# First layer of a four-layer block: two 32-token blocks swapped in every second tile, and a block-wise triangular solve in three stages over four diagonal array tiles

## What is computed

```python
q = silu(x @ Wq.T); k = silu(x @ Wk.T); v = x @ Wv.T        # 16 heads of 32
beta = 2.0 * sigmoid(x @ Wbeta.T)
k = k * rsqrt(sum(k * k) + EPS)
def step(S, inp):                                            # one token after the other
    qt, kt, vt, bt = inp
    pred = einsum('bhk,bhkv->bhv', kt, S)
    delta = bt[..., None] * (vt - pred)
    S = S + einsum('bhk,bhv->bhkv', kt, delta)
    o = einsum('bhk,bhkv->bhv', qt, S)
    return (S, o)
gate = sigmoid(x @ Wg1.T @ Wg2.T); og = o * gate
og = og * rsqrt(mean(og * og) + EPS) * g_norm;  return og @ Wo.T
```

## Time and profile before

| | us |
|---|---|
| median of three runs | 4828.01 (4825.08 to 4836.86) |
| the profiled execution, its own time | 4826.68 |
| its span in the profile | 4824.6 |
| first layer, start of the span to about | 1860 |
| mean granted clock of TensorE | 0.978 of full speed |

### The profile page before, as it was taken

How to read it: one execution, slowest core, us unless ns; L and a number is a source line. 1 busy time by engine, 2 the same in 40 slices (tenths; PEclk the granted TensorE clock), 3 DMA queues, 4 the chain that set the end, 5 groups by cost and what they waited for, 6 DMA issues and landing times.

```text
span 4824.6 us, 144788 instructions
## 1 busy us (share of the span) xinstructions
PE 4466.7 (93%) x63104; PEld 3089.8 (64%) x63104; DVE 3603.4 (75%) x7890; ACT 2416.7 (50%) x4592; POOL 707.2 (15%) x909
## 2 busy tenths in 40 slices
PE   7999999999999985999999999999999999999998
PEld 6777777777887764565565565565565565565564
DVE  5777767777777773877877877877877877877876
ACT  3344444434444332646646646646646646645645
POOL 0000000000000001122122122122122122122121
PEclk8999999999999997999999999999999999999999
DMA  2223222222322222000000000000000000000000
GB/s 88 56 74 75 73 69 65 65 69 74 78 69 65 65 65 80 1 18 1 19 18 2 19 19 2 19 19 2 19 18 2 19 18 2 19 18 2 19 10 10
DMA packets 352135, 171.76 MB, mean 36 GB/s; under 512 B 300017, under 2 KB 300785, under 8 KB 350737
## 3 DMA queue, kind: packets, MB, share of 16 engines
q1 hardware_dynamic: 342528, 145.20, 11.3%
q10 hardware_dynamic: 8976, 17.30, 1.3%
HBM read 93.74 MB, written 67.63 MB: 33 GB/s over the span
## 4 chain that ended last, share of the span: by engine, by line
PE 45%; DVE 11%; ACT 2%; issue 1%; POOL 1%; DMA 1%; SPq 0%; DVEq 0%; ACTq 0%; POOLq 0%
PE row_psum L1720 10%; PE row_psum L1745 10%; PE row_psum L40 5%; PE row_psum L42 5%; PE row_psum L41 5%; DVE smax L2007 5%; PE row_psum L1733 4%; PE row_psum L1793 1%; DVE xr_lo L1868 1%; PE row_psum L1773 1%; DVE probs L1987 1%; PE row_psum L1507 1%; DVE stats L1834 1%; POOL rstd L1304 1%; PE row_psum L1692 1%
## 5 line engine op out<-in xcount | busy, mean ns | idle before, releaser
L2007 DVE TENSOR_REDUCE smax<-row_psum 128x1 f32<-128x512 f32 x2048 | 1270.5, 681 | 94.8 <-PE row_psum L1720 93.7
L1441 ACT ACTIVATE probs<-row_psum 128x512 f32<-128x512 f32 x2048 | 1090.7, 602 | 350.0 <-PE row_psum L1733 330.5
L1720 PE MATMUL row_psum<-k_stack,q_stack 64*128 64x512 f32 (+1 forms) x2048 | 740.5, 440 | 50.6 <-DVE smax L2007 24.4
L1733 PE MATMUL row_psum<-q_stack,k_stack 64*128 64x512 f32 (+1 forms) x2048 | 733.5, 458 | 20.3 <-ACT probs L1441 8.1
L1720 PEld LDWEIGHTS row_psum<-k_stack,q_stack 64*128 64x128 f32 (+1 forms) x2048 | 354.3, 188 | 499.3 <-DVE smax L2007 367.9
L1745 PE MATMUL row_psum<-probs,v_aug 128*32 128x512 f32 x4096 | 538.9, 603 | 1.7 <-ACT av_sb L1457 0.4
L1733 PEld LDWEIGHTS row_psum<-q_stack,k_stack 64*128 64x128 f32 (+1 forms) x2048 | 319.2, 184 | 223.3 <-ACT probs L1441 155.7
L894 DVE TENSOR_TENSOR lane_t<-lane_t,lane_p 128x30 f32<-128x30 f32 (+14 forms) x960 | 318.3, 332 | 33.0
L40 PE MATMUL row_psum<-wf_hi,xr_hi 128*128 128x320 f32 (+1 forms) x1024 | 332.0, 324 | 5.3 <-DVE xr_lo L1868 3.2
L891 DVE TENSOR_TENSOR lane_p<-lane_t 128x30 f32<-128x30 f32 (+14 forms) x960 | 316.0, 329 | 25.5
L42 PE MATMUL row_psum<-wf_hi,xr_lo 128*128 128x320 f32 (+1 forms) x1024 | 319.0, 312 | 0.0
(11 more groups left out here) (215 smaller groups left out, 9854.2 us busy)
## 6 DMA issues: line engine op xcount, KB each, us to landing
x_sp<-in_x ACTq DMA_DIRECT2D x33, 512.0 KB, 4.3
tri_dram<-tri SPq DMA_DIRECT2D x256, 64.0 KB, 3.2
lane_t<-tri_dram SPq DMA_DIRECT2D x32, 512.0 KB, 3.8
inv_dram<-lane_t SPq DMA_DIRECT2D x32, 512.0 KB, 2.7
inv_b<-inv_dram SPq DMA_DIRECT2D x256, 64.0 KB, 2.3
x_res<-in_x SPq DMA_DIRECT2D x32, 512.0 KB, 3.9
x<-x_res SPq DMA_DIRECT2D x32, 512.0 KB, 3.2
xs<-x SPq DMA_DIRECT2D x16, 1024.0 KB, 5.5
```

The costliest lines, as they stand in the source:

```text
L1441: act.activation(probs[:, h % PROBS, tt, :], ps[:, m % STACK_BANKS, :], ACT.Exp, scale=float(DH) ** -0.5).then_inc(exp_ready, 1)
L1720: pe.matmul(ps[:, bank, :], q_stack[rows, qt, P * st:P * st + P], k_stack[rows, kv, :], start=True, stop=True).then_inc(max_mm, 1)
L1733: pe.matmul(ps[:, m % STACK_BANKS, :], k_stack[rows, kv, P * tt:P * tt + P], q_stack[rows, qt, :], start=True, stop=True).then_inc(score_m ...
L2007: dve.tensor_reduce(smax[:, g, st:st + 1], ps[:, bank_of("max", NT * g + st), :], AX.X, ALU.max).then_inc(max_ready, 1)
```

## The change

Tile 1 of every span gets its two 32-token blocks swapped in each chunk: its early block now lies on partitions 32 to 63 and 96 to 127. `upper` of tile 1 then uses array tiles (1,1) and (3,3), `product` (1,0) and (3,2), `under` (0,0) and (2,2). The four solve stages become three, `solve_upper`, `solve_product` and `solve_under`, each with all four quarters (128 records), in which tile 0's and tile 1's matmuls alternate: four array tiles with no row and no column in common.

- `turned` does tile 1's four blocks as fp32 matmuls with a swapped identity where it had transposes.
- The queries and the gate go back to token order when ScalarE reads them: `take_q` and `take_gate` become three activations for each one (256, 128 and 128 elements a partition).
- Tile 1's triangles use a swapped mask. The swapped identity and mask are loaded by 4 and 12 small DMAs on SP's queue, ahead of later weight loads; `first_in` and `c_in` count them.
- `solve_upper` waits for the third mask operation of tile 1 before its first matmul, and for the fourth before its second half.
- ScalarE takes the quarters in the order 0, 2, 1, 3, and all four `take_upper` before `take_k(further, 0)`; VectorE does all four corrections before it inverts columns 1 to 4.

```diff
+IN_TURN = (0, 2, 1, 3)
+def turn(q): return IN_TURN.index(q) + 1
+def blocks_of(ap, t, h):
+    if t == 0:
+        return ap[:, :, 0:P]
+    return ap[:, :, P:2 * P].rearrange("p g (c h r) -> p g c h r", c=2, h=2)[:, :, :, h, :]
+def in_token_order():
+    return ((0, None), (0, None)), ((1, 0), (1, 1)), ((1, 1), (1, 0))
...
             sp.dma_start(ident[:, :], ident_in).then_inc(first_in, 16)
+            for pb in range(P // NB):
+                sp.dma_start(ident_swapped[NB * pb:NB * pb + NB, :],
+                             ident_in[NB * (pb ^ 1):NB * (pb ^ 1) + NB, :]).then_inc(first_in, 16)
...
             sp.dma_start(masks[:, :], masks_in).then_inc(c_in, 16)
+            for pb in range(P // NB):
+                rows, other = slice(NB * pb, NB * pb + NB), slice(NB * (pb ^ 1), NB * (pb ^ 1) + NB)
+                sp.dma_start(masks_swapped[rows, 0:NB], masks_in[other, NB:2 * NB]).then_inc(c_in, 16)
+                sp.dma_start(masks_swapped[rows, NB:2 * NB], masks_in[other, 0:NB]).then_inc(c_in, 16)
+                sp.dma_start(masks_swapped[rows, C:2 * C], masks_in[other, C:2 * C]).then_inc(c_in, 16)
...
 def take_q(b, s, n):
-    act.activation(kq[:, 2 * n:2 * n + 2, 1 + s, :], (BA, BC)[n][:, :].rearrange("p (g i) -> p g i", g=2),
-                   ACT.Silu).then_inc(q_ready, 1)
+    for place, tokens in in_token_order():
+        last = act.activation(blocks_of(kq[:, 2 * n:2 * n + 2, 1 + s, :], *tokens),
+                              blocks_of((BA, BC)[n][:, :].rearrange("p (g i) -> p g i", g=2), *place), ACT.Silu)
+    last.then_inc(q_ready, 1)
 # take_gate likewise, ACT.Tanh
...
 # turned
+    if t:
+        last = pe.matmul(into, xn[:, t, P * k:P * k + P], ident_swapped[:, :], start=True, stop=True)
+    else:
+        last = pe.transpose(into, xn[:, t, P * k:P * k + P], ident[:, :])
...
+def block(t, half, late):
+    first = 2 * NB * half + NB * (late if t == 0 else 1 - late)
+    return slice(first, first + NB)
...
+def both_tiles(stage, b, s, n, done):
+    for i in range(H):
+        last = [stage(b, s, 2 * t + n, i) for t in range(TS)]
+    for ins in last:
+        ins.then_inc(done, 1)
+def solve_upper(b, s, ahead):
+    for n in range(2):
+        if ahead:
+            pe.wait_ge(tri_ready, at(*ahead, TS * HPT, HPT + n + 3))
+        both_tiles(upper, b, s, n, u0_mm)
+def solve_product(b, s):
+    for n in range(2):
+        pe.wait_ge(u0_ready, at(b, s, 2 * TS, 2 * n + 2))
+        both_tiles(product, b, s, n, p_mm)
+def solve_under(b, s):
+    for n in range(2):
+        pe.wait_ge(rhs2_ready, at(b, s, 2 * TS, 2 * n + 2))
+        both_tiles(under, b, s, n, u1_mm)
...
 # TensorE's step
-    solve_first(*now, ahead);  project_k(*further, 0);  solve_second(*now, ahead)
-    project_k(*further, 1);  solve_third(*now);  project_q(*further, 0)
-    solve_fourth(*now);  project_gb(*further)
+    solve_upper(*now, ahead);  project_k(*further, 0);  solve_product(*now)
+    project_k(*further, 1);  solve_under(*now);  project_q(*further, 0);  project_gb(*further)
...
 # VectorE's step
-    correct_lower(*now, 0, behind);  correct_lower(*now, 1, behind)
+    for q in IN_TURN:
+        correct_lower(*now, q, behind)
     invert_ahead("split")
     invert_ahead("product")
-    correct_lower(*now, 2, behind);  correct_lower(*now, 3, behind)
```

More of the change, by code:

```diff
@@ L325, in take_gate @@
                     act.wait_ge(gate_proj, at(b, s, 2, n + 1))
-                    act.activation(gate[:, s, 2 * n:2 * n + 2, :], (BA, BB)[n][:, :], ACT.Tanh, scale=0.5).then_inc(gate_ready, 1)
+                    for place, tokens in in_token_order():
+                        last = act.activation(blocks_of(gate[:, s, 2 * n:2 * n + 2, :], *tokens),
+                                              blocks_of((BA, BB)[n][:, :].rearrange("p (g i) -> p g i", g=2), *place),
+                                              ACT.Tanh, scale=0.5)
+                    last.then_inc(gate_ready, 1)
             def k_inverse_norms(b, s):
@@ L422, in step @@
                     turned(*further)
-                take_upper(*now, 0)
-                take_upper(*now, 1)
+                for q in IN_TURN:
+                    take_upper(*now, q)
                 if further:
                     take_k(*further, 0)
-                take_upper(*now, 2)
-                take_upper(*now, 3)
-                if further:
                     take_k(*further, 1)
-                for q in range(2 * TS):
+                for q in IN_TURN:
                     take_lower(*now, q)
@@ L586, in product @@
                 h, half = 8 * n + i // 2, i % 2
-                r = slice(2 * NB * half, 2 * NB * half + NB)
-                return pe.matmul(bank[4 + q][2 * NB * half + NB:2 * NB * half + 2 * NB, 2 * HD * (h % 8):2 * HD * (h % 8) + 2 * HD],
-                                 tri[r, s, t, h // HPT, h % HPT, NB:2 * NB], uw[r, t, h, :], start=True, stop=True)
+                r = block(t, half, 0)
+                return pe.matmul(bank[4 + q][block(t, half, 1), 2 * HD * (h % 8):2 * HD * (h % 8) + 2 * HD],
+                                 tri[r, s, t, h // HPT, h % HPT, NB * (1 - t):NB * (1 - t) + NB], uw[r, t, h, :], start=True, stop=True)
             def under(b, s, q, i):
@@ L594, in under @@
                 h, half = 8 * n + i // 2, i % 2
-                r = slice(2 * NB * half + NB, 2 * NB * half + 2 * NB)
+                r = block(t, half, 1)
                 return pe.matmul(bank[4 + q][r, 2 * HD * (h % 8):2 * HD * (h % 8) + 2 * HD],
                                  inv_b[r, t, h, :], rhs2[r, t, h, :], start=True, stop=True)
-            def solve_first(b, s, ahead):
+            def both_tiles(stage, b, s, n, done):
[4 more added lines that the diff above has]
+            def solve_upper(b, s, ahead):
                 pe.wait_ge(inv_in, at(b, s, 16 * TS * 4, 16 * TS * 4))
@@ L770, in step @@
                     turned(*further)
-                solve_first(*now, ahead)
+                solve_upper(*now, ahead)
                 if further:
                     project_k(*further, 0)
-                solve_second(*now, ahead)
+                solve_product(*now)
                 if further:
                     project_k(*further, 1)
-                solve_third(*now)
+                solve_under(*now)
                 if further:
                     project_q(*further, 0)
-                solve_fourth(*now)
-                if further:
                     project_gb(*further)
@@ L995, in step @@
                     split_x(*further)
-                correct_lower(*now, 0, behind)
-                correct_lower(*now, 1, behind)
+                for q in IN_TURN:
+                    correct_lower(*now, q, behind)
                 invert_ahead("split")
                 invert_ahead("product")
-                correct_lower(*now, 2, behind)
-                correct_lower(*now, 3, behind)
                 if further:
```

57 lines of the change are left out of this document (16 added, 41 removed).

## The result

The changed kernel takes 4805.84 us (median of five runs, 4795.07 to 4812.91) against 4828.01 for the kernel before. The ratio is 0.9948, with an interval of 0.9936 to 0.9960: about 25 us faster. The kernel before has five executions by now as well, with the same median (4824.45 to 4836.86). The profiled execution is the fastest of the five, 4795.07 us with a span of 4793.3, 31.3 shorter than the span before.

What follows compares the result with a forecast made beforehand. TensorE, busy 93% of the span, was taken to bound the kernel. Middle steps -24 us, the end -5 and the start +3 make -26 us, from 4826.7 to a predicted 4801 us, range 4780 to 4824.

Steps and rivals of the forecast that it cites:

- The stages: Solve in a middle step: a stage of 128 records takes 2.0 us (1.9 to 2.2); three replace four, saving 1.90 us.
- rival E: Solve stages: row tiles sharing a PSUM bank take turns, about 4 us a stage, 4.9 us a step lost, 4972 us; 2%.
- The start: Step's start to `project_k`: `turned` 1.6 us, covered by the mask wait, solve at T0 + 2.1; 0.82 us lost ahead of `project_k`.
- The gate: `take_gate` on ScalarE, on the path to `key_rows`: 1.35 us for 1.07, 0.28 us more a step.
- Rival B: ScalarE and `turned`: small operations overlap less or fp32 matmuls do not hide, taking the gain back; 4817 to 4826 us; 18%.
- The middle step: Each of 30 middle steps: 1.08 us gained to `query_corrections`, 0.28 lost at the gate; 0.80 us net, 24 us in all.
- The end: Last step but one: all four corrections come before the lanes, VectorE then sets `advance`; about 5 us gained, bounds 2 and 8.
- The start of the kernel: Prologue: 16 DMAs delay the last weight loads, 1 us, and two spans pay `turned` and gate uncovered, 2 us; 3 us lost.
- A: Whole kernel: the forecast itself holds, 4785 to 4813 us; 55%.
- F: Middle steps: stops without a releaser happen to fall into waits, 0.4 us a step less, 4770 to 4785 us; 9%.
- Rival C: TensorE in middle steps: the denser solve adds a stop without a releaser, 0.8 us a step, cancelling the gain, 4825 us; 10%.
- Rival D: At `key_rows`: the longer 0.9 us wait drops the clock to 1.2 GHz, 1.7 us each time, 4852 us if every step; 6%.

Runs made afterwards that it cites:

- third experiment: Changed kernel, but VectorE corrects quarters 0 and 2 before inverting columns 1 to 4, and 1 and 3 after; 4916.92 us, ratio 1.0189.
- second trace: The changed kernel run once more without any edit, for another trace; 4794.17 us, ratio 0.9948 to the kernel before.
- swap alone: Changed kernel with blocks still swapped, but the solve back to four stages and the old orders; 4824.46 us, ratio 1.0006 to the kernel before.

## Why the prediction came out right

Point by point, by the first profile after:

- **The stages.** Taken at 2.0 us, they take 1.92, all three. Four array tiles on the diagonal have the pace of the mixed stages of before, 15 ns a record. The bank rule (rival E) is refuted: rows 0 and 2 write one bank at full pace.
- **The start.** `turned` 1.55 us (forecast 1.6, covered), the solve at T0 + 2.09 (2.1), `project_k` at T0 + 4.01 (4.1), `query_corrections` at T0 + 18.23. The forecast 18.7 started from a step whose stages were longer than most. Steps without a stop had 19.52 us there, so the gain is 1.29 us, not 1.08.
- **The gate.** 0.24 us on ScalarE (0.28), and the same 0.24 at `key_rows` (0.62 and 0.86 us in most steps). Rival B has no part in it: six pieces take 1.31 us where they would have 1.89 without overlap.
- **VectorE.** The four corrections end within 0.2 us of the lanes' landing, so the inversion does not wait, and the third experiment shows what their place is worth: some 110 us.
- **The middle step.** 0.80 us forecast, 23.7/30 = 0.79 measured. That is partly luck. The net time goes from 1611.8 to 1585.7 us, 0.87 a step. The stops took 9 us (42.8 to 51.6), and 6 came back in the clock.
- **The end.** 5 us forecast. In the last step but one, VectorE goes from its masked triangles to its first `advance` in 31.9 us instead of 36.7, without a wait before it, and TensorE waits 2.2 us for it: 4.8 us, by the mechanism forecast. The 6.2 above start at the solve, which itself starts 1.2 us later there, behind the third mask operation.
- **The start of the kernel.** 3 us lost were forecast, and 1.4 gained measured, 0.1 in the second trace. The term has the wrong sign. ScalarE did wait 1.4 us for the third weight (0.5 in the second trace), but the first `project_k` took 3.2 us where it had taken 5.1, at the higher clock; in the second trace it took 4.4. That part is the luck of the clock.

The sum of the terms was 26, the medians say 22 and the ratio 25. The chances do not add up as written: A, F and a third of B and C make 0.73 for faster, not 0.71.

Rival C, the stops, is real at a third of its price. Their sum is 7 to 9 us higher than in the one trace of before, and the new ones stand where the program has become dense, in `solve_upper` and behind it. There they are up to 2.3 us long (2.8 in the second trace), because TensorE has used up its block before the late transfer of the next one has landed. Why the transfer is late is open: less lane traffic took 3 us at most off these stops. Loads of the inverses, which come just ahead of the solve, were not tried. Rival D, the clock, did not happen at `key_rows`: beside none of its 29 waits (0.9 us) does the clock fall. It did beside longer holes, in the third experiment.

## What to carry to other kernels

Count how many array tiles are at work in each stage of small matmuls, and read the records' pace from the trace. For these fp32 matmuls of 32x32 with 64 columns it went with that number, 30 ns a record for two and 15 for four, whether the tiles shared rows, columns or banks or not. A change of layout that keeps four at work throughout is paid at its borders, so look for the border off the critical chain (here g1 and not the gate). When an order is changed, move the other engines' work of that stage with it: it was worth four times the change.

## What was not expected of the hardware

TensorE's stops without a releaser are waits for its own instructions. Each of the 808 stops in the middle steps of twelve traces stands at the same remainder of the instruction's number by 256, and ends 1.2 to 1.8 us after a 16384-byte instruction transfer has landed. 53 of 65 stood before the same matmul in two executions; they moved by 32 matmul records when 64 instructions were put ahead of the loop, and kept their sum (51.6 us). In the twelve traces that sum is 34 to 67 us of about 1650, and among the kernels whose net step is near that of before it tends to be larger where that step is shorter. So an edit that is worth 10 us can be given or lost by it: the swap alone looked free.
